# The weighted accumulation of a mixture-of-experts stage, on GpSimd in two instructions in place of one on VectorE

## The chip, the cores and the metric

The kernel runs on one core of one Trainium2 chip. Its time is the device time of the whole program in microseconds (us); a comparison takes the median of several executions. TensorE is PE in the profile, VectorE is DVE, ScalarE is ACT, GpSimd is POOL, SyncE is SP.

## The reference

One decoder layer over `x` of 2 x 256 tokens by 128 features: self-attention, a second attention with a causal and a cross part, and an expert stage, each followed by a residual and a layer norm. The change touches the expert stage alone:

```python
gate_scores = softmax(einsum('btd,ed->bte', x, Wg))
topk_val, topk_idx = top_k(gate_scores, 2)
topk_val = topk_val / (topk_val.sum(-1, keepdims=True) + 1e-9)
comb = (one_hot(topk_idx, 8) * topk_val[..., None]).sum(-2)
out = zeros_like(x)
for e in range(8):
    h = einsum('btd,hd->bth', x, W1[e]) + b1[e]        # 512 columns
    a, b = split(h, 2, axis=-1)
    eo = einsum('bth,dh->btd', a * sigmoid(b), Wo) + bo
    out = out + eo * comb[..., e:e + 1]
x = layernorm(x + out)
```

All experts share `Wo`, so the kernel sums `a * sigmoid(b)` over the experts with the weights of `comb`, and multiplies by `Wo` once.

## The kernel before

The kernel is written engine by engine, with semaphores. A function `plan()` makes one list of steps, `steps`, and each engine's block walks this list in order and issues its own part of each step. So the order of the steps is the order in every engine's queue, and an instruction that waits holds back all that stands behind it on its engine.

The two batches (b = 0, 1) have two token tiles of 128 each (t = 0, 1). The steps of the expert stage are:

- `GATE b`: TensorE makes the gate's logits, ScalarE their exponentials, and VectorE goes through some twenty small instructions (L784 to L811) that end in `comb`, the weight of each token for each expert, kept in `gate[:, b, 10]`.
- `F b e t`: one expert for one token tile, 32 in all. TensorE multiplies the tile with `w1T` (L600, two records by the two parts of an fp32 product) and adds the bias (L601). The result stands in PSUM, in `w0` or `w1` for even e and in `t0` or `t1` for odd e, so four products can be on their way. ScalarE takes the tanh of one half into `tanh_b` (L926; sigmoid is written with tanh, and the factor of one half is in the weights), which has four slots. VectorE makes the gated product `(tanh + 1) * a` into `gated` (L819, the rows call it `val_qc`), which has two slots, and frees the PSUM buffer. Then it adds the product times its weight to `gsum` (the rows call it `ctx_room`): L832 for e = 0, L835 for the seven others.
- `GT b t`: TensorE transposes the finished sum (L608), VectorE copies it out of PSUM (L840).
- `OUT b t`: TensorE multiplies by `Wo` (L615), VectorE adds the residual (L844) and takes the variance (L641, L644), GpSimd raises it to the power -0.5 (L995, L996), and VectorE normalizes (L651). SyncE stores.

`m` is one PSUM buffer for all of transposes, gate and output products; the next of them waits until VectorE has emptied it.

The items F are counted n = 0 to 31 in the order of the list. It runs: n = 0 to 7 are batch 0, tile 0, with the last attention steps of batch 1 among them (`TY`, `YT` and `WO`: its values normalized by L732, L734 and L737, transposed by L552, multiplied by L560; then the layer norm `LN`, L651 twice, behind n = 7). Items 8 and 9 are batch 0, tile 1, e = 0 and 1. Then `XT` (transpose, copied out by L760) and `GATE` of batch 1. Items 10 to 17 are batch 1, tile 0; 18 and 19 are batch 1, tile 1, e = 0 and 1; `GT 0 0`; 20; `GT 1 0`; 21; `OUT 0 0`; 22 to 26 (batch 0, tile 1); `OUT 1 0`; 27 to 31 (batch 1, tile 1); `GT 0 1`; `OUT 0 1`; `GT 1 1`; `OUT 1 1`.

GpSimd has nothing to do in this stage but L995 and L996.

## Time and profile before

| | us |
|---|---|
| median of 3 runs (271.98 to 272.28) | 272.1 |
| the profiled execution: from its first to its last instruction (its span) | 266.8 |
| the median less this span | 5.3 |
| busy in the span: PE / DVE / ACT / POOL | 195.4 / 176.4 / 91.5 / 57.7 |
| the expert items F, from the first L600 to the last product | 197.6 to 257.1 |

For the profiled execution the profile gives the span alone; the 5.3 us are what lies around it. Busy time is the time in which an engine executed something, and of an engine that is not the last to end a wait it says little. In the stretch from 198 us to the end, TensorE is busy nearly all the time; the rows in the last section but one show where it is not. A timeline row gives the start, the busy time, the engine and line, the operation with output <- input, and in brackets how long the engine had been idle and what ended that.

### The profile page before, as it was taken

To read this page: it belongs to the slowest core of one execution; us is meant where nothing else is said; L and a number is where in the kernel's file an instruction comes from. 1 tells how busy PE (TensorE), PEld (TensorE's weight loads), DVE (VectorE), ACT (ScalarE), POOL (GpSimd) and SP (SyncE) were. 2 spreads that over 40 slices of the span, in tenths; PEclk is the share of its full clock that TensorE was granted. 3 is DMA by queue.
4 is the path that set the end of the run, shared out by engine and by line. 5 is a ranking of instruction groups with operands and counts; after the bars stand their busy time and mean duration, and the time that the engine had idled before them with its cause. 6 is when DMAs were issued, how large, how long until landed. Compare 5 with 4: busy or idle time off the path is not lost.

```text
span 266.8 us, 3648 instructions
## 1 busy us (share of the span) xinstructions
PE 195.4 (73%) x1280; PEld 89.6 (34%) x1280; DVE 176.4 (66%) x423; ACT 91.5 (34%) x138; POOL 57.7 (22%) x85
## 2 busy tenths in 40 slices
PE   4605800878976085349978999999999997999961
PEld 2301100322335053134424343566555422233321
DVE  4999921498447089517888798897432686867762
ACT  4500000547740001013507485666765222222210
POOL 8993005940136017500000000001000010001101
PEclk9855555599999579559989999999999997999995
DMA  6339998000016645840000000000000000000000
GB/s 147 50 55 101 117 142 345 4 0 4 2 24 56 61 43 72 75 35 4 2 2 0 4 0 2 2 4 2 6 0 2 0 0 4 0 0 11 8 2 20
DMA packets 8117, 9.41 MB, mean 35 GB/s; under 512 B 1380, under 2 KB 6940, under 8 KB 7972
## 3 DMA queue, kind: packets, MB, share of 16 engines
q1 hardware_dynamic: 6660, 6.82, 14.8%
q0 software_dynamic: 1440, 2.37, 8.1%
q8 instruction: 10, 0.16, 0.3%
q14 instruction: 7, 0.06, 0.1%
HBM read 4.02 MB, written 0.26 MB: 16 GB/s over the span
## 4 chain that ended last, share of the span: by engine, by line
PE 51%; DVE 24%; DMA 16%; issue 3%; SPq 3%; ACT 2%; POOL 0%; POOLq 0%; ACTq 0%; DVEq 0%
PE y L527 11%; DVE mneg L694 11%; DMA q_stack_A<-mrow 6%; PE t L600 6%; PE w L600 6%; PE w L451 4%; DMA k_stack_b<-part_k 4%; PE t L496 4%; DMA q_stack_B<-mrow 4%; DVE part_q L634 3%; SPq L377 2%; PE t L478 2%; PE t L485 2%; PE w L601 2%; PE t L601 2%
## 5 line engine op out<-in xcount | busy, mean ns | idle before, releaser
L694 DVE TENSOR_REDUCE mneg<-w 128x1 f32<-128x512 f32 (+2 forms) x128 | 78.4, 651 | 38.8 <-PE w L441 14.8
L886 ACT ACTIVATE probs<-t 128x1024 f32<-128x1024 f32 x48 | 48.4, 1023 | 64.6 <-PE t L478 41.6
L995 POOL TENSOR_SCALAR rstd<-mv 128x2 f32<-128x2 f32 (+1 forms) x8 | 1.8, 224 | 165.3 <-DVE mv L644 165.3
L441 PE MATMUL w<-k_stack_a,q_stack_A 128*128 128x256 bf16 x64 | 16.3, 363 | 20.3 <-DMA q_stack_A<-part_q 15.7
L451 PE MATMUL w<-k_stack_c,q_stack_A 128*128 128x512 bf16 x64 | 25.1, 409 | 4.1 <-DVE mneg L694 3.5
L883 ACT ACTIVATE probs<-t 128x768 f32<-128x768 f32 x16 | 12.8, 810 | 24.2 <-PE t L490 24.2
L496 PE MATMUL t<-q_stack_A,k_stack_c 128*128 128x256 bf16 x128 | 19.7, 278 | 0.4 <-ACT probs L886 0.3
L527 PE MATMUL y<-probs,v_c 128*32 128x256 f32 x256 | 19.0, 388 | 0.3 <-issue 0.2
L600 PE MATMUL t<-w1T,xT 128*128 128x512 f32 x32 | 18.5, 660 | 0.0
L600 PE MATMUL w<-w1T,xT 128*128 128x512 f32 x32 | 18.2, 652 | 0.0
L441 PEld LDWEIGHTS w<-k_stack_a,q_stack_A 128*128 128x128 bf16 x64 | 5.1, 111 | 33.1 <-DMA q_stack_A<-part_q 17.0
L444 PE MATMUL w<-k_stack_b,q_stack_B 128*128 128x128 bf16 x32 | 7.7, 240 | 11.0 <-DMA k_stack_b<-part_k 7.6
L478 PE MATMUL t<-q_stack_A,k_stack_a 128*128 128x512 bf16 x32 | 10.8, 432 | 6.6 <-DMA q_stack_A<-mrow 6.5
L485 PE MATMUL t<-q_stack_B,k_stack_b 128*128 128x256 bf16 x32 | 9.6, 300 | 7.5 <-DMA q_stack_B<-mrow 7.2
L835 DVE SCALAR_TENSOR_TENSOR ctx_room<-val_qc,gate,ctx_room 128x256 f32<-128x256 f32 x28 | 13.6, 486 | 1.0
L496 PEld LDWEIGHTS t<-q_stack_A,k_stack_c 128*128 128x128 bf16 x128 | 11.7, 99 | 7.2 <-issue 5.0
L819 DVE SCALAR_TENSOR_TENSOR val_qc<-val_qk,w 128x256 f32<-128x256 f32 x16 | 6.7, 420 | 9.6 <-ACT val_qk L926 9.5
L926 ACT ACTIVATE val_qk<-t 128x256 f32<-128x256 f32 x16 | 6.1, 383 | 18.6 <-PE t L601 18.6
L451 PEld LDWEIGHTS w<-k_stack_c,q_stack_A 128*128 128x128 bf16 x64 | 6.2, 98 | 18.2 <-DVE mneg L694 13.6
L819 DVE SCALAR_TENSOR_TENSOR val_qc<-val_qk,t 128x256 f32<-128x256 f32 x16 | 6.7, 417 | 8.3 <-ACT val_qk L926 8.2
L926 ACT ACTIVATE val_qk<-w 128x256 f32<-128x256 f32 x16 | 6.1, 383 | 17.0 <-PE w L601 17.0
L897 ACT ACTIVATE y_sb<-y 128x512 f32<-128x512 f32 x12 | 7.2, 596 | 11.3 <-PE y L527 11.2
(168 smaller groups left out, 336.6 us busy)
## 6 DMA issues: line engine op xcount, KB each, us to landing
w1T<-in_w1T SPq DMA_DIRECT2D x1, 2048.0 KB, 19.5
k_stack_c<-y_sb POOLq DMA_DIRECT2D x6, 256.0 KB, 12.3
rest<-in_rest SPq DMA_DIRECT2D x1, 772.0 KB, 15.4
q_stack_A<-part_q SPq DMA_DIRECT2D x12, 64.0 KB
q_stack_B<-part_q SPq DMA_DIRECT2D x12, 64.0 KB
bias_row<-in_rows SPq DMA_DIRECT2D x1, 384.0 KB, 7.3
k_stack_b<-part_k POOLq DMA_DIRECT2D x6, 64.0 KB, 6.2
k_stack_b<-part_k SPq DMA_DIRECT2D x6, 64.0 KB
```

The source lines that it names most:

```text
L441: last = nc.tensor.matmul(o[:, i * T:(i + 1) * T], q[:, head, q0 + i * P:q0 + (i + 1) * P], k_stack_a[:, q0:q0 + T], start=True, stop=True)
L451: last = nc.tensor.matmul(o[:], q[:, head, q0 + qt * P:q0 + (qt + 1) * P], k_stack_c[:, head, b * TC:(b + 1) * TC], start=True, stop=True)
L478: last = nc.tensor.matmul(o[:, kt * 512:(kt + 1) * 512], k_stack_a[:, q0 + kt * P:q0 + (kt + 1) * P], rhs, start=True, stop=True)
L485: nc.tensor.matmul(o[:, c0:c0 + T], k_stack_b[:, head, q0:q0 + P], q[:, head, q0:q0 + T], start=True, stop=False)
L496: last = nc.tensor.matmul(o[:, kt * T:(kt + 1) * T], k_stack_c[:, head, k0:k0 + P], q[:, head, q0:q0 + T], start=True, stop=True)
L527: last = nc.tensor.matmul(y_open[32 * j:32 * j + VW, cols], v, p, start=(kt == 0), stop=(kt == last_kt[part]), tile_position=(0, 32 * j))
L600: nc.tensor.matmul(o, x2T[:, b * T + t * P:b * T + (t + 1) * P], w1T[:, e, :], start=True, stop=False)
L694: emptied(V.tensor_reduce(out=dst, in_=src, axis=AX.X, op=ALU.max, negate=True), s)
L819: emptied(V.scalar_tensor_tensor(out=product, in0=tanh_b[:, n % 4, :], scalar=1.0, in1=o[:, 0:HF], op0=ALU.add, op1=ALU.mult), s)
L835: ins = V.scalar_tensor_tensor(out=dst, in0=product, scalar=weight, in1=dst, op0=ALU.mult, op1=ALU.add)
L883: ins = A.activation(dst.rearrange("p (i c) -> p i c", i=2)[:, :, 0:T + P], o[:].rearrange("p (i c) -> p i c", i=2)[:, :, 0:T + P], ACT.Exp)
L886: ins = A.activation(dst, o[:], ACT.Exp)
```

## The change

VectorE keeps the gated product (now L823) and no longer weighs or adds. GpSimd does it: for e = 0 one multiplication by the weight into the sum, for the seven others a multiplication into a scratch tile `weighed` (in the old room of `part_qc`) and an addition to the sum. Each of GpSimd's pair waits for the one before. Four waits are new: GpSimd waits for the product (the semaphore that also frees the PSUM buffer), for `comb` at e = 0, and after each addition for itself; VectorE waits, before the product of item n, until GpSimd has finished item n - 2, since `gated` has two slots.

```diff
+        weighed = part_qc[:, 0:2, :].bitcast(F32).rearrange("p a n -> p (a n)").rearrange("p (a n) -> p a n", n=HF)
...
-                    link(V.tensor_tensor(t["comb"], t["one0"], t["one1"], ALU.add))
+                    V.tensor_tensor(t["comb"], t["one0"], t["one1"], ALU.add).then_inc(s_comb, 1)
+                    dve.wait_ge(s_comb, b + 1)
...
+                    if n >= 2:
+                        dve.wait_ge(s_gated, n - 1)
...
-                    wait_emptied(dve, s)
-                    dst = gsum[:, b, t, :]
-                    weight = gate[:, b, 10, t, e:e + 1]
-                    if e == 0:
-                        ins = V.tensor_scalar(dst, product, weight, None, ALU.mult)
-                    else:
-                        dve.wait_ge(s_gated, n)
-                        ins = V.scalar_tensor_tensor(out=dst, in0=product, scalar=weight, in1=dst,
-                                                     op0=ALU.mult, op1=ALU.add)
-                    ins.then_inc(s_gated, 1)
...
+                elif kind == "F":
+                    _, b, e, t = s
+                    n = f_of[s[1:]]
+                    wait_emptied(pool, s)
+                    if n == 0:
+                        pool.wait_ge(s_stack["qC0"], STACKED)
+                        pool.wait_ge(s_stack["qC1"], STACKED)
+                    dst = gsum[:, b, t, :]
+                    weight = gate[:, b, 10, t, e:e + 1]
+                    if e == 0:
+                        pool.wait_ge(s_comb, b + 1)
+                        G.tensor_scalar(dst, gated[:, n % 2, :], weight, None, ALU.mult).then_inc(s_gated, 1)
+                    else:
+                        link(G.tensor_scalar(weighed[:, n % 2, :], gated[:, n % 2, :], weight, None, ALU.mult))
+                        G.tensor_tensor(dst, dst, weighed[:, n % 2, :], ALU.add).then_inc(s_gated, 1)
+                        pool.wait_ge(s_gated, n + 1)
```

The queue of VectorE from `GT 1 0` to item 22, before. `part_k<-m` is the copy of `GT 1 0`, `z`, `stats`, `mv` and `rest` are `OUT 0 0`:

```order
L819 SCALAR_TENSOR_TENSOR val_qc<-val_qk,w0 128x256 [waits full_w0,tanh_done]
L835 SCALAR_TENSOR_TENSOR ctx_room<-val_qc,gate,ctx_room 128x256 [waits gated_sum,free_w0]
L840 COPY part_k<-m 128x256 [waits full_m]
L819 SCALAR_TENSOR_TENSOR val_qc<-val_qk,w1 128x256 [waits full_w1,tanh_done]
L835 SCALAR_TENSOR_TENSOR ctx_room<-val_qc,gate,ctx_room 128x256 [waits gated_sum,free_w1]
L844 TENSOR_TENSOR z<-m,xpb 128x128 [waits full_m]
L641 BN_STATS stats<-z 128x6 [waits free_m]
L644 BN_AGGR mv<-stats 128x2 [waits chain_dve]
L651 TENSOR_SCALAR rest<-z,mv,rstd 128x128 [waits rstd]
L819 SCALAR_TENSOR_TENSOR val_qc<-val_qk,t1 128x256 [waits full_t1,tanh_done]
L835 SCALAR_TENSOR_TENSOR ctx_room<-val_qc,gate,ctx_room 128x256 [waits gated_sum,free_t1]
```

The same place of VectorE's queue with the change, down to the same item:

```order
L823 SCALAR_TENSOR_TENSOR val_qc<-val_qk,w0 128x256 [waits gated_sum,full_w0,tanh_done]
L834 COPY part_k<-m 128x256 [waits full_m]
L823 SCALAR_TENSOR_TENSOR val_qc<-val_qk,w1 128x256 [waits gated_sum,full_w1,tanh_done]
L838 TENSOR_TENSOR z<-m,xpb 128x128 [waits full_m]
L642 BN_STATS stats<-z 128x6 [waits free_m]
L645 BN_AGGR mv<-stats 128x2 [waits chain_dve]
L652 TENSOR_SCALAR rest<-z,mv,rstd 128x128 [waits rstd]
L823 SCALAR_TENSOR_TENSOR val_qc<-val_qk,t1 128x256 [waits gated_sum,full_t1,tanh_done]
```

The three L835 are gone, and each product waits for `gated_sum`, the count that GpSimd now makes.

GpSimd's queue from the same `OUT 0 0` on, before: the pairs of three `OUT` steps follow each other, and each waits for its own variance.

```order
L995 TENSOR_SCALAR rstd<-mv 128x1 [waits variance]
L996 TENSOR_TENSOR rstd<-rstd,half_neg 128x1 [waits chain_pool]
L995 TENSOR_SCALAR rstd<-mv 128x1 [waits variance]
L996 TENSOR_TENSOR rstd<-rstd,half_neg 128x1 [waits chain_pool]
L995 TENSOR_SCALAR rstd<-mv 128x1 [waits variance]
L996 TENSOR_TENSOR rstd<-rstd,half_neg 128x1 [waits chain_pool]
```

With the change, GpSimd's queue from item 20 to item 23 (`free_w0` and the like are the product's semaphores, `variance` is that of `OUT 0 0`):

```order
L1005 TENSOR_SCALAR part_qc<-val_qc,gate 128x256 [waits free_w0,gated_sum]
L1006 TENSOR_TENSOR ctx_room<-ctx_room,part_qc 128x256 [waits chain_pool]
L1005 TENSOR_SCALAR part_qc<-val_qc,gate 128x256 [waits free_w1,gated_sum]
L1006 TENSOR_TENSOR ctx_room<-ctx_room,part_qc 128x256 [waits chain_pool]
L989 TENSOR_SCALAR rstd<-mv 128x1 [waits variance,gated_sum]
L990 TENSOR_TENSOR rstd<-rstd,half_neg 128x1 [waits chain_pool]
L1005 TENSOR_SCALAR part_qc<-val_qc,gate 128x256 [waits free_t1]
L1006 TENSOR_TENSOR ctx_room<-ctx_room,part_qc 128x256 [waits chain_pool]
L1005 TENSOR_SCALAR part_qc<-val_qc,gate 128x256 [waits free_w0,gated_sum]
L1006 TENSOR_TENSOR ctx_room<-ctx_room,part_qc 128x256 [waits chain_pool]
```

The power of `OUT 0 0` now stands behind item 21 on GpSimd, that of `OUT 1 0` behind item 26, and that of `OUT 0 1` behind item 31; before, nothing stood ahead of them.

## Rows read from the trace of the kernel before

**Rows 1.** One window: busy PE, PEld, DVE, ACT, POOL (instructions), granted clock, DMA, GB/s

```profile
230.00:238.00 8.00, 8.00 (x19) 2.09 (x18) 5.60 (x13) 2.19 (x6) 0.00 (x0) 1.00 0.00 0
```

**Rows 2.** Timeline (start, us, what): two of TensorE's items, VectorE's sum

```profile
231.09 1.12 PE L600 MATMUL t<-w1T,xT 128*128 128x512 f32 x2
232.47 1.12 PE L600 MATMUL w<-w1T,xT 128*128 128x512 f32 x2
233.50 0.48 DVE L835 SCALAR_TENSOR_TENSOR ctx_room<-val_qc,gate,ctx_room 128x256 f32<-128x256 f32 x1
```

**Rows 3.** Timeline, VectorE ahead of the transpose of batch 1's attention

```profile
209.16 0.42 DVE L819 SCALAR_TENSOR_TENSOR val_qc<-val_qk,w 128x256 f32<-128x256 f32 x1 [1.29 <-ACT val_qk L926]
210.86 0.42 DVE L737 TENSOR_TENSOR ytok<-ytok 128x256 f32<-128x256 f32 x1
```

**Rows 4.** Timeline, from item 9 to the gate's product of batch 1

```profile
221.24 0.48 DVE L835 SCALAR_TENSOR_TENSOR ctx_room<-val_qc,gate,ctx_room 128x256 f32<-128x256 f32 x1
221.64 0.42 DVE L760 COPY xT<-m 128x256 f32<-128x256 f32 x1
222.21 0.58 PE L590 MATMUL m<-rest,xT 128*128 128x8 f32 x4 [1.56 <-DVE xT L760]
```

**Rows 5.** Timeline, from item 19 to `GT 1 0`

```profile
239.00 0.48 DVE L835 SCALAR_TENSOR_TENSOR ctx_room<-val_qc,gate,ctx_room 128x256 f32<-128x256 f32 x1
239.40 0.42 DVE L840 COPY part_q<-m 128x256 f32<-128x256 f32 x1
239.96 0.41 PE L608 MATMUL m<-ident,ctx_room 128*128 128x128 f32 x2 [0.39 <-DVE part_q L840]
```

**Rows 6.** Timeline, GpSimd: an addition and a cast of 256 columns

```profile
78.28 0.67 POOL L941 TENSOR_TENSOR val_qk<-val_qk,part_k 128x256 f32<-128x256 f32 x1 [3.67 <-ACT val_qk L912]
79.02 0.47 POOL L942 CAST part_k<-val_qk 128x256 bf16<-128x256 f32 x1
```

**Rows 7.** GpSimd's groups by form: busy us, mean ns of one

```profile
L1003 POOL TENSOR_TENSOR xpb<-x,bias_row 128x128 f32<-128x128 f32 x4 | 1.7, 455 | 9.3 <-DVE x L651 9.3
L995 POOL TENSOR_SCALAR rstd<-mv 128x2 f32<-128x2 f32 x4 | 0.9, 227 | 120.9 <-DVE mv L644 120.9
```

**Rows 8.** VectorE, a cast in the timeline and L832 among its groups

```profile
77.97 0.29 DVE L634 CAST part_q<-val_qk 128x256 bf16<-128x256 f32 x1
L832 DVE TENSOR_SCALAR ctx_room<-val_qc,gate 128x256 f32<-128x256 f32 x4 | 1.4, 354 | 0.1
```

**Rows 9.** Timeline, from item 21 through `OUT 0 0` to item 22

```profile
242.06 0.42 DVE L819 SCALAR_TENSOR_TENSOR val_qc<-val_qk,w 128x256 f32<-128x256 f32 x1 [0.70 <-ACT val_qk L926]
243.84 0.23 POOL L995 TENSOR_SCALAR rstd<-mv 128x1 f32<-128x1 f32 x1 [27.20 <-DVE mv L644]
244.76 0.34 DVE L651 TENSOR_SCALAR rest<-z,mv,rstd 128x128 f32<-128x128 f32 x1 [1.00 <-POOL rstd L996]
245.02 0.41 DVE L819 SCALAR_TENSOR_TENSOR val_qc<-val_qk,t 128x256 f32<-128x256 f32 x1
```

**Rows 10.** Timeline, GpSimd at `OUT 1 0`

```profile
251.16 0.22 POOL L995 TENSOR_SCALAR rstd<-mv 128x1 f32<-128x1 f32 x1 [6.43 <-DVE mv L644]
```

**Rows 11.** Timeline, the copy of `GT 0 1` and the norm of `OUT 0 1`

```profile
257.55 0.42 DVE L840 COPY part_q<-m 128x256 f32<-128x256 f32 x1
260.65 0.34 DVE L651 TENSOR_SCALAR rest<-z,mv,rstd 128x128 f32<-128x128 f32 x1 [0.98 <-POOL rstd L996]
```

**Rows 12.** Timeline, a VectorE cast beside a GpSimd memset

```profile
4.87 6.92 POOL L961 MEMSET k_stack_c<- 128x8192 f32 x1
6.25 6.84 DVE L634 CAST part_q<-val_qk 128x256 bf16<-128x256 f32 x1
```

**Rows 13.** TensorE's window behind the gate (busy, granted clock, DMA, GB/s)

```profile
222.90:226.50 3.60, 3.60 (x5) 0.53 0.02 7
```

**Rows 14.** Timeline, one of TensorE's items in that window, and product 10

```profile
224.74 1.99 PE L600 MATMUL t<-w1T,xT 128*128 128x512 f32 x2
227.30 0.42 DVE L819 SCALAR_TENSOR_TENSOR val_qc<-val_qk,w 128x256 f32<-128x256 f32 x1
```

More of the change, by code:

```diff
@@ L333, in build @@
         s_ytok, s_xres, s_var, s_rstd, s_xn = map(sem, ("y_normed", "residual_ready", "variance", "rstd", "x_normed"))
-        s_lmax, s_tanh, s_gated, s_fin, s_store = map(
-            sem, ("gate_max", "tanh_done", "gated_sum", "fin_ready", "stored"))
+        s_lmax, s_comb, s_tanh, s_gated, s_fin, s_store = map(
+            sem, ("gate_max", "gate_weights", "tanh_done", "gated_sum", "fin_ready", "stored"))
         block = stack.enter_context(nc.Block())
```

## The prediction

> **What bounds the kernel now.** I read the slices of the whole span first, then the chain of work that ended last, then the list of waits, and at last the timeline of the expert stage. The chain shows that the stage from 212 us on is TensorE's: in the window from 230 to 238 us TensorE is busy for 8.00 of 8.00 us, VectorE for 5.60, GpSimd for nothing [rows 1]. An item F starts every 1.38 us on TensorE (232.47 less 231.09), and VectorE's part of it, product and sum, takes some 0.9 us [rows 2]. So there the sum that the change takes off VectorE is hidden, and its removal brings nothing. It counts only where TensorE waits for VectorE with a sum in front. The waits and the timeline show four such places: ahead of the transpose of batch 1's attention [rows 3], at the gate's product [rows 4], at GT 1 0 [rows 5], and in the tail, from the copy of GT 0 1 at 257.55 on, where VectorE, TensorE and GpSimd follow each other without cover [rows 11]. A fifth kind of place is the norm in OUT, where VectorE waits 1.00 us for GpSimd's power [rows 9].
>
> **What is removed.** 28 sums L835 of 0.48 us and four L832 of 0.354 us leave VectorE [rows 2, 8]. Of these 15 us, the path sees:
> - Gate: L760 would start at 221.24, where L835 stood, in place of 221.64, and TensorE, idle for 1.56 us and released by it, starts 0.40 us earlier [rows 4].
> - GT 1 0: L840 starts at 239.00 in place of 239.40, again 0.40 us, since TensorE waits 0.39 us for it [rows 5].
> - Ahead of the transpose of batch 1's attention L737 (start 210.86) could come 0.40 us earlier. Against this stands a lock. At the kernel's start a VectorE cast that elsewhere takes 0.29 us [rows 8] took 6.84 us, from 6.25 on, and ended about 1.3 us behind a GpSimd memset that ran from 4.87 for 6.92 us [rows 12]: a VectorE operation of some kinds stands still beside a busy GpSimd. L737 has two inputs in SBUF. Product 2 ends at 209.58 [rows 3]; GpSimd's pair for it would run until about 210.95, so L737 would end near 211.3 where it ended at 211.28. I take +0.05 us here (bounds: -0.40 without a lock, +0.15 with it).
>
> The Trainium skill (SBUF — State Buffer, Who interferes with whom) says that the pair of ports that VectorE and GpSimd share is an exclusive lock, taken by a VectorE instruction with two SBUF inputs or in a two-port mode, and that the loser stands still for a whole instruction. The trace agrees in the 6.84 us; without the rule the sum would be 0.4 us lower. Products read PSUM and one SBUF tensor, so by that page they never take the lock.
>
> **What is added on GpSimd.** Per item, a multiplication by a per-token weight, 128x256, and an addition of two fp32 tiles of the same size. The addition: with 128 columns 0.455 us, and a fixed part of 0.227 us from an operation on two columns [rows 7], so 2 x 0.455 - 0.227 = 0.68 us; the addition of 256 columns with one bf16 input took 0.67 [rows 6]. Between dependent instructions lie 0.07 us (78.95 to 79.02) [rows 6]; I take 0.08 ahead of the addition and 0.07 behind. The multiplication by a weight that is read from memory is not in the trace on GpSimd. Its lower bound is the fixed 0.227 us and 254 columns at the memset's 0.84 ns (6.92 us for 8192): 0.44 us [rows 7, 12]. Its upper bound is the two-input addition, 0.68. Nearest is the cast of 256 columns, also one input and one output, 0.47 us [rows 6]; on VectorE the weight makes L832 0.354 where a cast takes 0.29 [rows 8], so I add 0.06 and take 0.53 us. One item then costs GpSimd r = 0.53 + 0.08 + 0.68 + 0.07 = 1.36 us, with bounds of 1.26 and 1.51. TensorE's pace is 1.38. So GpSimd is full: it follows, but can catch up on nothing.
>
> The Trainium skill (GPSIMD Engine Reference, Performance versus the Vector engine) gives a best case of about 1.8 cycles per element for a one-input loop at 1.2 GHz, and calls VectorE the engine for elementwise work. That is an estimate of 0.23 + 256 x 1.5 ns = 0.61 us for the multiplication, r = 1.44, and the sum below would be 273.4 in place of 272.5. No row here has this operation; the cast of rows 6 is cheaper than the page's rate.
>
> **What moves.** GpSimd walks the same list, so each power (L995, L996) now stands behind the item in front of it, and VectorE's norm, with the next products queued behind it, waits for both. This decides the end. I walk it in the old clock times, the shifts of TensorE left out:
> - Product 21 starts at 242.06 and ends at 242.48 [rows 9]; GpSimd has it from 242.56 to 243.92 (r). The variance is now ready 0.44 us earlier, but the power starts at 243.92, where it started at 243.84 [rows 9]. The saved sum is eaten by the wait for GpSimd.
> - From the power's start to the norm's start 0.92 us, to product 22 another 0.26 [rows 9], product and hand-over 0.50: GpSimd starts item 22 at 245.60. Items 22 to 26 queue up in front of the power of OUT 1 0: 5 x 1.36 = 6.80, so it starts at 252.40, where it started at 251.16 [rows 10]. VectorE stands in the norm for that time, with products 27 and on behind it.
> - Again 0.92 + 0.26 + 0.50 = 1.68: GpSimd starts item 27 at 254.08, and has 31 done at 260.88. Only then comes the power of OUT 0 1, and the norm 0.92 later, at 261.80. Before, it stood at 260.65 [rows 11]. VectorE's copy of GT 1 1 stands behind this norm, and the rest of the kernel behind the copy.
>
> In short, the norm of OUT 0 1 comes at 246.84 + 11 r. With r = 1.36 that is 1.15 us late, although the copy of GT 0 1 alone would have come 0.40 early. Four PSUM buffers hide all this from TensorE: item 31 needs the buffer of item 27, and product 27 ends near 254.0, before TensorE comes to item 31. For item 10 the new wait for comb costs nothing, since VectorE makes both in order. The four e = 0 items cost GpSimd one instruction (0.60 us), by which the small backlog behind the layer norm and the gate is worked off ahead of item 20.
>
> **The sum.** -0.40 (gate) - 0.40 (GT 1 0) + 0.05 (transpose) + 1.15 (tail) = +0.40 us. The profiled span of 266.8 becomes 267.2, and with the 5.3 us around it the median of 272.1 becomes 272.5.
>
> **The rivals.**
> - **GpSimd is slower than TensorE's pace.** The multiplication costs as much as the two-input addition: r = 1.51, the norm at 263.45, 2.80 us late, sum +2.05, time 274.1. For it: GpSimd does this in a software loop, and one more operand must be fetched. Against it: the cast. It decides from r = 1.37 on, where the sum passes +0.54. Anything at or above a multiplication of 0.54 us is measurably slower.
> - **The pair is cheap.** With r = 1.26 the norm stands at 260.70, 0.05 late, and the sum is -0.70: 271.4. The turn from faster to slower is at r = 1.32, a multiplication of 0.49 us.
> - **The clock stays up.** Behind the gate's wait of 1.56 us TensorE's granted clock was 0.53 for 3.60 us [rows 13], that is mostly at 1.2 in place of 2.4 GHz, and two matmuls took 1.99 us [rows 14] where they take 1.12 [rows 2]. At full clock the same work takes 1.9 us, so up to 1.7 us, some 1.4 on the path, are lost there. The wait shortens to 1.16 us, and the drop may not come. GpSimd would give back a part: product 10 is bound to the gate's chain on VectorE (227.30, now 226.90) [rows 14], and from 227.40 GpSimd has ten pairs and two single items to the power of OUT 0 0, 14.8 us, until 242.2; the forecast has 243.92 - 0.80 = 243.1. So 0.9 us at r = 1.36: 271.6. With r = 1.26 all of the 1.4 would count, 270.0.
> - **VectorE's saving isn't on any path**, and GpSimd keeps up: no change, 272.1. The two waits of rows 4 and 5 speak against it; it falls within the same band.
>
> **Chances.** Forecast (multiplication of 0.47 to 0.57 us, clock as before) 0.34; slow GpSimd 0.32; cheap pair 0.18; clock 0.13; something else that costs, such as more locking, 0.03. A change of less than 0.2% (0.54 us) can't be told from none. Faster: most of the clock case and half of the cheap pair, 0.21. Slower: the slow case, and the upper part of the forecast's own span, 0.42. Within 0.2%: the rest, 0.37. The range reaches from the clock case with a cheaper pair, 270.9, to the slow case with 0.5 us of blocking more, 274.6.
>
> **What would show it.** Right: GpSimd about 97% busy from item 22 to 31 with r near 1.36, the multiplication at 0.53 us, the power of OUT 1 0 and OUT 0 1 directly behind an addition, VectorE idle for more than 2 us in the norm of OUT 1 0, the gate's product 0.4 us earlier. Wrong: a multiplication far from 0.53, or TensorE held by a full PSUM buffer in the stage's middle, or a granted clock of 1.00 behind the gate.

## The result

The changed kernel takes 281.3 us (279.7 to 284.7, 4 runs) where the kernel before took 272.0 on the same chip (271.5 to 272.3, 4 runs): ratio 1.035, 95% interval 1.025 to 1.044. The prediction was 272.5 with a range of 270.9 to 274.6. It named the right side and the right places in the tail, and was far too small: an instruction was sized too cheap, and with its real size GpSimd sets the pace in a stretch where the prediction let TensorE lead.

Executions of one kernel differ here by several us, some faster and some slower, and much of this lies ahead of the expert stage, which starts anywhere from 196.5 to 202.6 us in the fourteen profiles. So the experiments are read by the **stage**: from the start of the first expert product on TensorE (L600, in the changed kernel L601) to the start of the last norm (L651, now L652). Before, 197.62 to 264.52 = 66.9 us; changed, 196.45 to 275.14 = 78.7 us, so 11.8 us more. (The two spans, 266.8 and 277.4 us, differ by 10.6, since this stage starts 1.2 us earlier.) A second trace of the changed kernel, and one of the kernel before with instructions added ahead of the stage, give 78.7 and 66.9 again.

One thing varies in the stage beside the change: how long TensorE stays at the lower of its two clock levels (1.2 in place of 2.4 GHz) behind the gate. It is 3.4 us in the kernel before and 6.8 in the changed one; two kernels below that differ in little else show what 3.4 us more of it cost where TensorE leads: 1.7 us. A difference between two stages of that size says nothing before the clock has been looked at.

The groups of GpSimd in the changed kernel, by form (busy us, mean ns of one | idle time before them and its releaser):

```profile
L1005 POOL TENSOR_SCALAR part_qc<-val_qc,gate 128x256 f32<-128x256 f32 x28 | 26.0, 928 | 11.5 <-DVE val_qc L823 9.8
L1006 POOL TENSOR_TENSOR ctx_room<-ctx_room,part_qc 128x256 f32<-128x256 f32 x28 | 20.3, 726 | 2.3
L1003 POOL TENSOR_SCALAR ctx_room<-val_qc,gate 128x256 f32<-128x256 f32 x4 | 3.7, 926 | 19.2 <-DVE val_qc L823 19.0
```

The multiplication by the weight takes 0.93 us, where the prediction took 0.53 and at most 0.68. The addition, 0.73, is near the 0.68 that was worked out. The timeline of GpSimd and VectorE in the stretch that answers to [rows 1] and [rows 2]:

```profile
230.91 0.92 POOL L1005 TENSOR_SCALAR part_qc<-val_qc,gate 128x256 f32<-128x256 f32 x1 [0.33 <-DVE val_qc L823]
...
232.74 0.92 POOL L1005 TENSOR_SCALAR part_qc<-val_qc,gate 128x256 f32<-128x256 f32 x1
233.75 0.72 POOL L1006 TENSOR_TENSOR ctx_room<-ctx_room,part_qc 128x256 f32<-128x256 f32 x1
...
234.60 0.42 DVE L823 SCALAR_TENSOR_TENSOR val_qc<-val_qk,t 128x256 f32<-128x256 f32 x1 [1.18 <-POOL ctx_room L1006]
```

A pair starts every 232.74 - 230.91 = 1.83 us (0.93 + 0.08 + 0.72 + 0.10), against TensorE's pace of 1.38 [rows 2], and VectorE waits for GpSimd before a product. The next view gives one long window, with the columns of [rows 1]: from item 10's instruction on GpSimd to the power of `OUT 0 1`.

```profile
227.90:270.25 42.35, 33.90 (x78) 11.30 (x78) 13.32 (x37) 8.04 (x21) 36.41 (x46) 0.86 0.01 3
```

GpSimd is busy for 36.4 of 42.35 us. The rest is four waits, 2.4 us together, and the short gaps between its 46 instructions. TensorE, which had no idle time there before but at `GT` and `OUT`, is idle for 8.4 us. The list of waits from 204 us on says the same (total us, times, longest):

```profile
DVE val_qc L823 <- POOL ctx_room L1006: 16.1, 12, 1.7
...
DVE rest L652 <- POOL rstd L990: 7.7, 4, 3.4
PEld m L616 <- DVE part_q L834: 4.9, 1, 4.9
PE m L616 <- DVE part_q L834: 4.7, 1, 4.7
```

And the chain that ended last, shares of the whole span by engine; POOL had no share in it before:

```profile
PE 40%; DVE 22%; DMA 15%; POOL 13%; issue 4%; SPq 2%; ACT 2%; POOLq 0%; another core or an unknown queue 0%; DVEq 0%; ACTq 0%
```

**Where the 11.8 us arise.** The powers and norms are the marks, in the timeline of the changed kernel. They answer to [rows 9 to 11]:

```profile
248.64 0.23 POOL L989 TENSOR_SCALAR rstd<-mv 128x1 f32<-128x1 f32 x1
...
259.50 0.23 POOL L989 TENSOR_SCALAR rstd<-mv 128x1 f32<-128x1 f32 x1
...
270.34 0.22 POOL L989 TENSOR_SCALAR rstd<-mv 128x1 f32<-128x1 f32 x1
...
271.25 0.34 DVE L652 TENSOR_SCALAR rest<-z,mv,rstd 128x128 f32<-128x128 f32 x1 [1.55 <-POOL rstd L990]
```

Counted from the stage's start, the power of `OUT 0 0` is at 52.19 us (before 46.22), 5.97 late. To the power of `OUT 1 0` it takes 10.86 us (before 7.32), 3.54 more, and to that of `OUT 0 1` 10.84, 2.24 more. Each of the three powers starts right behind an addition. So the two stretches of five items cost about what the walk gives with r = 1.83 in it (0.92 + 0.26 + 0.50 + 5 x 1.83 = 10.83). The 5.97 us ahead of item 22 are what the walk didn't hold.

There, already the gate comes late, in the rows that answer to [rows 4]:

```profile
221.05 0.42 DVE L823 SCALAR_TENSOR_TENSOR val_qc<-val_qk,t 128x256 f32<-128x256 f32 x1 [1.40 <-POOL ctx_room L1006]
221.39 0.42 DVE L761 COPY xT<-m 128x256 f32<-128x256 f32 x1
...
221.95 0.86 PE L591 MATMUL m<-rest,xT 128*128 128x8 f32 x4 [2.73 <-DVE xT L761]
```

The copy is no longer behind a sum, but behind product 9, which waits for GpSimd's item 7. TensorE waits 2.73 us in place of 1.56, and its product is 0.91 us later from the stage's start (25.50, before 24.59). Product 10, behind the gate's chain, is 1.2 us late (227.32 - 196.45 = 30.87; before 29.68 by [rows 14]). From there the items 10 to 21 go through GpSimd at its own pace, with a single wait of 0.33 us, and take 4.8 us more than before; so the longer low clock of TensorE can't have cost more than that third of a microsecond here. At `GT 1 0` [rows 5] the same thing happens:

```profile
241.92 0.42 DVE L823 SCALAR_TENSOR_TENSOR val_qc<-val_qk,t 128x256 f32<-128x256 f32 x1 [1.41 <-POOL ctx_room L1006]
242.26 0.42 DVE L834 COPY part_q<-m 128x256 f32<-128x256 f32 x1
...
242.82 0.66 PE L609 MATMUL m<-ident,ctx_room 128*128 128x128 f32 x2 [1.92 <-POOL ctx_room L1003]
```

TensorE waits 1.92 us where it waited 0.39.

### The profile page after: what moved, and what is told of

Same layout as the page of the kernel before. It is cut to its first block, busy times and chain, and to the rows that moved or that the text cites. A ratio compares the mean times of both kernels' runs of the same rounds, so it can differ in the third digit from the quotient of the medians.

```text
span 277.4 us, 3673 instructions
## 1 busy us (share of the span) xinstructions
PE 197.6 (71%) x1272; PEld 91.5 (33%) x1280; DVE 162.7 (59%) x391; ACT 91.4 (33%) x138; POOL 107.8 (39%) x145
## 4 chain that ended last, share of the span: by engine, by line
PE 40%; DVE 22%; DMA 15%; POOL 13%; issue 4%; SPq 2%; ACT 2%; POOLq 0%; another core or an unknown queue 0%; DVEq 0%; ACTq 0%
DVE mneg L695 11%; PE y L528 10%; POOL part_qc L1005 6%; DMA q_stack_A<-mrow 6%; POOL ctx_room L1006 5%; DMA k_stack_b<-part_k 4%; DMA q_stack_B<-mrow 4%; PE t L497 4%; PE w L601 3%; PE w L452 3%; DVE part_q L635 3%; SPq L378 2%; PE t L479 2%; PE t L486 2%; PE t L601 2%
## 5 line engine op out<-in xcount | busy, mean ns | idle before, releaser
L1005 POOL TENSOR_SCALAR part_qc<-val_qc,gate 128x256 f32<-128x256 f32 x28 | 26.0, 928 | 11.5 <-DVE val_qc L823 9.8
L452 PE MATMUL w<-k_stack_c,q_stack_A 128*128 128x512 bf16 x56 | 21.2, 390 | 4.6 <-DVE mneg L695 4.0
L1006 POOL TENSOR_TENSOR ctx_room<-ctx_room,part_qc 128x256 f32<-128x256 f32 x28 | 20.3, 726 | 2.3
L601 PE MATMUL w<-w1T,xT 128*128 128x512 f32 x32 | 20.3, 719 | 0.0
L601 PE MATMUL t<-w1T,xT 128*128 128x512 f32 x32 | 19.4, 692 | 0.4 <-DVE val_qc L823 0.4
L823 DVE SCALAR_TENSOR_TENSOR val_qc<-val_qk,t 128x256 f32<-128x256 f32 x16 | 6.7, 421 | 19.5 <-POOL ctx_room L1006 9.9
L823 DVE SCALAR_TENSOR_TENSOR val_qc<-val_qk,w 128x256 f32<-128x256 f32 x16 | 6.7, 421 | 19.4 <-ACT val_qk L920 12.9
L479 PE MATMUL t<-q_stack_A,k_stack_a 128*128 128x512 bf16 x32 | 10.6, 426 | 6.4 <-DMA q_stack_A<-mrow 6.4
```

The costliest lines, as they stand in the source:

```text
L452: last = nc.tensor.matmul(o[:], q[:, head, q0 + qt * P:q0 + (qt + 1) * P], k_stack_c[:, head, b * TC:(b + 1) * TC], start=True, stop=True)
L479: last = nc.tensor.matmul(o[:, kt * 512:(kt + 1) * 512], k_stack_a[:, q0 + kt * P:q0 + (kt + 1) * P], rhs, start=True, stop=True)
L601: nc.tensor.matmul(o, x2T[:, b * T + t * P:b * T + (t + 1) * P], w1T[:, e, :], start=True, stop=False)
L823: emptied(V.scalar_tensor_tensor(out=product, in0=tanh_b[:, n % 4, :], scalar=1.0, in1=o[:, 0:HF], op0=ALU.add, op1=ALU.mult), s)
L1005: link(G.tensor_scalar(weighed[:, n % 2, :], gated[:, n % 2, :], weight, None, ALU.mult))
L1006: G.tensor_tensor(dst, dst, weighed[:, n % 2, :], ALU.add).then_inc(s_gated, 1)
```

## The experiments

The expectations name four theories. A: GpSimd's time per item, 1.83 us against TensorE's pace of 1.38, makes the loss. B: GpSimd's and VectorE's memory accesses slow each other. C: the powers, queued behind items, make it. D: the added waits and the queue order cost, however long an instruction takes.

### The changed kernel again

No edit.

> The changed kernel once more, for the spread of its time and a second trace. Theory A (GpSimd's throughput: an item costs it 1.83 us, more than TensorE's 1.38) expects the multiplication at 0.92 us and the addition at 0.72 again, whatever the state of the rest, and a time of 279 to 283 us. Theory B (the two engines disturb each other on the memory ports, so that the multiplication is stretched) expects multiplications that vary with what VectorE does beside them. Theory C (the powers behind the items are what costs) expects most of the loss in VectorE's waits for the power.

Measured: 280.7 us (279.8 to 285.0), ratio 1.037 (1.023 to 1.052), stage 78.7 us, L1005 928 ns, L1006 726, as theory A expects. The stage repeats to 0.1 us.

### A constant in place of the weight

```diff
-                        link(G.tensor_scalar(weighed[:, n % 2, :], gated[:, n % 2, :], weight, None, ALU.mult))
+                        link(G.tensor_scalar(weighed[:, n % 2, :], gated[:, n % 2, :], 0.125, None, ALU.mult))
```

(L1003 likewise.) The gate's weights are left out of the sum.

> The weight read from memory is replaced by the constant 0.125 in GpSimd's multiplication, which leaves the gate's weights out of the sum; everything else is as in the changed kernel. If the fetch of the per-token weight is what makes the multiplication 0.92 us, it falls to 0.45 to 0.55 us, an item to some 1.35 us and the time to 272 to 273 us (theory A with the price of the forecast). If the operation costs that much with any second operand, the time stays at 280. Theory B expects it to stay near 0.92, since VectorE does the same beside it.

Measured: 280.4 us (277.7 to 284.0), stage 75.7, 3.0 less. The group of L1005 by form:

```profile
L1005 POOL TENSOR_SCALAR part_qc<-val_qc 128x256 f32<-128x256 f32 x28 | 23.9, 853 | 10.9 <-DVE val_qc L823 9.3
```

The weight from memory costs 0.075 us, about the 0.06 that the prediction added for it. The other 0.85 us is what the instruction costs with no second operand at all. So "one input and one output" was the wrong likeness.

### The weight as a second tensor

```diff
-                        link(G.tensor_scalar(weighed[:, n % 2, :], gated[:, n % 2, :], weight, None, ALU.mult))
+                        link(G.tensor_tensor(weighed[:, n % 2, :], gated[:, n % 2, :], weight.to_broadcast([P, HF]), ALU.mult))
```

(L1003 likewise.) The same values, in another form of instruction.

> GpSimd multiplies with a tensor operation in which the weight is read as a tensor of step 0, in place of the operation with a per-token scalar. The outputs are the same. Theory A: the multiplication costs what the addition does, 0.72 us, an item 1.62 us in place of 1.83; with some 21 items in the chain that is 3 to 4 us less, 276 to 277.5 us. Theory B: two tensors to read, so no cheaper, 280 or more. Theory C: no change worth naming.

Measured: 276.5 us (271.4 to 277.3), ratio 1.023 (1.014 to 1.033), stage 69.5.

```profile
L1005 POOL TENSOR_TENSOR part_qc<-val_qc,gate 128x256 f32<-128x256 f32 x28 | 17.3, 617 | 12.3 <-DVE val_qc L823 10.8
```

0.62 us in place of 0.93, so r = 0.62 + 0.08 + 0.72 + 0.08 = 1.50: the prediction's rival of a slow GpSimd, which had r = 1.51 and 2.05 us of loss. The stage shows 2.6, and from power to power 9.15 and 9.16 us (walk: 1.68 + 5 x 1.50 = 9.18). 9.2 of the 11.8 us go with one change of form. The profiled execution is the fastest of the five; the medians of the whole time, 276.5 and 280.7, show some 4 us of it. Theory A had the form at 0.72 us and r at 1.62: the direction was right, the price again taken from a likeness.

### The powers ahead of the item

```diff
+            pool_steps = list(steps)
...
+                if s in (("WO", 1, 1), ("OUT", 0, 0), ("OUT", 1, 0), ("OUT", 0, 1)):
+                    at = pool_steps.index(s)
+                    f = max(i for i in range(at) if pool_steps[i][0] == "F")
+                    pool_steps.insert(f, pool_steps.pop(at))
```

> On GpSimd alone, the power of four norms (of batch 1's attention and of the first three output steps) is put ahead of the item that stood in front of it; nothing else changes. Theory C: the loss goes with it, 273 to 275 us. Theory A: GpSimd's items still take their time, only the idle 0.8 us behind two powers and the last norm's wait for item 31 go, 2 to 3 us less, 277 to 279 us.

Measured: 283.7 us (282.8 to 286.6), stage 80.6, that is 1.9 us more than the changed kernel, where theory C had 273 to 275 us and theory A, which missed too, 277 to 279. GpSimd now stands still for the variance instead:

```profile
POOL rstd L995 <- DVE mv L645: 6.3, 3, 3.6
```

C falls: here GpSimd has no time to spare, and what it waits for in front of its work is lost. (The low clock behind the gate lasted 10.2 us in this profile, so the 1.9 us may not all be the order's.)

### VectorE multiplies, GpSimd adds

```diff
+                    V.tensor_scalar(weighed[:, n % 2, :], product, gate[:, b, 10, t, e:e + 1], None,
+                                    ALU.mult).then_inc(s_weighed, 1)
...
+                    if e == 0:
+                        G.tensor_copy(dst, weighed[:, n % 2, :]).then_inc(s_gated, 1)
+                    else:
+                        pool.wait_ge(s_gated, n)
+                        G.tensor_tensor(dst, dst, weighed[:, n % 2, :], ALU.add).then_inc(s_gated, 1)
```

> VectorE keeps the multiplication by the weight (into the scratch tile), GpSimd does the addition alone, and a copy for e = 0. The outputs are the same. Theory A: an item costs GpSimd 0.72 + 0.1 = 0.8 us, well under TensorE's 1.38, and VectorE 0.42 + 0.35 us; so nothing of the 9 us is left, 271.5 to 273 us, and TensorE is busy for the whole of a stretch in the stage's middle. Theory B (the engines disturb each other): VectorE's multiplication, which runs at two columns per cycle, meets GpSimd's addition in every item, and 3 us or more of the loss stay. Theory C (order): the powers stand behind the items as before, so most of the loss stays.

Measured: 271.2 us (10 runs), ratio 1.002 (0.997 to 1.007), stage 68.0. GpSimd has the same 28 additions of 0.724 us and the loss is gone but for 1.1 us, all of it there at the power of `OUT 0 0`; TensorE's low clock behind the gate lasted 6.8 us in this profile, which by itself is worth more. Theory B in its weak form is visible: VectorE's 32 multiplications take 352 to 642 ns, 388 on the mean, where L832 takes 354 alone [rows 8]. It costs no time that can be told.

### A probe of GpSimd's instructions in its idle time

In the kernel before, ahead of the stage, six operations on 64, 128 and 256 columns:

```diff
+                        for c in (64, 128, 256):
+                            a, o, q = first[0][:, 0:c], probe[:, 0:c], first[0][:, 256:256 + c]
+                            link(G.tensor_scalar(o, a, half_neg[:, 0:1], None, ALU.mult))
...
+                            link(G.tensor_tensor(o, a, half_neg[:, 0:1].to_broadcast([P, c]), ALU.mult))
+                            link(G.tensor_tensor(o, a, q, ALU.add))
+                            link(G.tensor_copy(o, a))
```

> The kernel before, with operations added on GpSimd where it is idle (behind 110 us), each waiting for the one before, at 64, 128 and 256 columns: multiplication by a per-partition scalar, by a constant, addition of a constant, multiplication by a tensor of step 0, addition of two tensors, copy. Theory A (the multiplication by a scalar is a slow loop of its own): 0.92, 0.85 and 0.85 us at 256 columns with nothing of weight beside it on VectorE, growing by more than 2 ns per column; the tensor forms 0.62 and 0.7, the copy 0.45. Theory B (stretched by VectorE's memory traffic): below 0.6 here, since VectorE reads PSUM at that time. The time of the kernel is not the question; some 13 us of GpSimd's idle time are used, and it should stay that of before.

Measured, by form (L1025 is the first line, L1028 to L1030 the last three):

```profile
L1025 POOL TENSOR_SCALAR probe<-first,half_neg 128x256 f32<-128x256 f32 x1 | 0.9, 927 | 0.1
...
L1029 POOL TENSOR_TENSOR probe<-first 128x256 f32<-128x256 f32 x1 | 0.7, 726 | 0.1
L1028 POOL TENSOR_TENSOR probe<-first,half_neg 128x256 f32<-128x256 f32 x1 | 0.6, 612 | 0.1
L1025 POOL TENSOR_SCALAR probe<-first,half_neg 128x128 f32<-128x128 f32 x1 | 0.6, 606 | 0.1
...
L1030 POOL COPY probe<-first 128x256 f32<-128x256 f32 x1 | 0.4, 397 | 0.1
```

The durations are those of the changed kernel to the nanosecond or two, though VectorE does other work here: B falls as a cause of the 0.93 us. Between 128 and 256 columns a TENSOR_SCALAR grows by 0.32 us, 2.5 ns a column; two tensors by (726 - 452) / 128 = 2.1 ns; the copy by (397 - 290) / 128 = 0.84 ns. Among these forms the copy is the cheapest by far (as the cast of [rows 6] is, 0.47 us), and TENSOR_SCALAR, which reads one tensor, is the slowest.

### The multiplication alone

```diff
-                        link(G.tensor_scalar(weighed[:, n % 2, :], gated[:, n % 2, :], weight, None, ALU.mult))
-                        G.tensor_tensor(dst, dst, weighed[:, n % 2, :], ALU.add).then_inc(s_gated, 1)
+                        G.tensor_scalar(dst, gated[:, n % 2, :], weight, None, ALU.mult).then_inc(s_gated, 1)
                         pool.wait_ge(s_gated, n + 1)
```

> The changed kernel without its 28 additions: GpSimd multiplies every product by its weight straight into the sum, in the same places of its queue and with the same waits; the sum over the experts is left out, the last expert's product stands for it. An item then costs GpSimd 0.93 us and 0.10 of hand-over, 1.03 us, though each multiplication takes as long as in the changed kernel. Theory A (GpSimd's time per item against TensorE's pace of 1.38 us, from the gate on): below the pace nothing is left of the loss; the stage from the first expert product to the last norm, 78.7 us in the changed kernel and 66.9 in the kernel before, takes 65.5 to 67.0, and the two gains of 0.4 us of the prediction (gate, GT 1 0) show. Theory B (VectorE is disturbed by GpSimd's memory accesses): GpSimd makes half of its instructions, so half of the loss stays, 71 to 74 us. Theory D (the waits between the two engines and the order of the queues cost, whatever an instruction takes): over 69 us.

Measured: 268.8 us, ratio 0.989 (0.981 to 0.996), stage 63.7, less than A's 65.5 to 67.0. All 28 slow multiplications are there (931 ns), and the loss has gone: D falls, and so does a B that would slow VectorE with every instruction of GpSimd. The gate's product starts 0.8 us earlier from the stage's start (23.82, before 24.59), with a wait of 1.05 us, and behind it the clock didn't fall, which brings the rest; see below.

### A copy in place of the multiplication

```diff
-                        link(G.tensor_scalar(weighed[:, n % 2, :], gated[:, n % 2, :], weight, None, ALU.mult))
+                        link(G.tensor_copy(weighed[:, n % 2, :], gated[:, n % 2, :]))
```

> The changed kernel with a copy of the product in place of its multiplication by the weight in the 28 pairs; the weights of experts 1 to 7 are left out of the sum. A copy of 256 columns takes GpSimd 0.40 us, so a pair takes 0.40 + 0.08 + 0.72 + 0.10 = 1.30 us. This is the case that the prediction's walk is made for, a pair a little below TensorE's pace of 1.38 us: the norm of OUT 0 1 at 246.84 + 11 x 1.30 = 261.14, 0.5 us late, and the sum -0.4 - 0.4 + 0.05 + 0.5 = -0.25 us. Theory A (the walk was right and only the multiplication was mis-sized): the stage takes 66.2 to 67.3 us (before 66.9, changed 78.7). Theory D (the structure of the pairs costs): over 68.5 us.

Measured: 269.6 us, ratio 0.994 (0.987 to 1.001), stage 67.8, half a microsecond above A's range. Copy 398 ns, addition 724, r = 1.30. From power to power 8.01 and 8.15 us (walk: 1.68 + 5 x 1.30 = 8.18). The clock was low for 6.8 us behind the gate, 3.4 us longer than before. By the 1.7 us that this costs elsewhere (an estimate here), the stage would be at 66.1, where the walk has 66.6. So with r below the pace the prediction's walk holds within half a microsecond.

### The first items, and the last ten

Two complements on the kernel before. The edit of one; the other has `n < 22 and s[2] > 0`.

```diff
+        MOVED = list(range(22, 32))
...
+                    if n in MOVED:
+                        continue
...
+                elif kind == "F" and f_of[s[1:]] in MOVED:
...
+                    G.tensor_scalar(weighed[:, n % 2, :], gated[:, n % 2, :], weight, None,
+                                    ALU.mult).then_inc(s_moved, 1)
+                    pool.wait_ge(s_moved, MOVED.index(n) + 1)
+                    pool.wait_ge(s_sum[(b, t)], e)
+                    G.tensor_tensor(dst, dst, weighed[:, n % 2, :], ALU.add).then_inc(s_sum[(b, t)], 1)
```

> The kernel before, with the two GpSimd instructions of the change for items 22 to 31 alone; items 0 to 21 are weighed and added by VectorE in one instruction. The walk of the prediction from the power of OUT 0 0 on, with r = 1.83 measured in the changed kernel: power of OUT 1 0 at 243.84 + 1.68 + 5 x 1.83 = 254.67 (before 251.16), power of OUT 0 1 at 265.50, its norm at 266.42 (before 260.65), 5.8 us late. Theory A: the stage takes 66.9 + 5.8 = 72.7 us (72 to 73.5). A rival in which only the whole run of 32 items matters (a backlog that fills up ahead of item 22 and is only handed on behind it) has 67 to 69 us here.

Measured, last ten: 277.5 us (276.8 to 281.2), ratio 1.022 (1.014 to 1.030), stage 74.2.

```profile
250.33 0.23 POOL L1007 TENSOR_SCALAR rstd<-mv 128x1 f32<-128x1 f32 x1 [28.42 <-DVE mv L649]
...
261.18 0.23 POOL L1007 TENSOR_SCALAR rstd<-mv 128x1 f32<-128x1 f32 x1
```

From power to power 10.85 and 10.84 us: with ten items alone each stretch costs what it costs in the changed kernel, 5.8 us together. Of the 7.3 us the other 1.5 lie ahead of item 22, where the instructions are those of the kernel before; there the clock was low for 6.8 us in place of 3.4. That is also why the stage is above the 72 to 73.5 that were expected.

> The complement of the kernel with the last ten: items below 22 with e > 0 by GpSimd's two instructions, all others by VectorE. In the changed kernel the power of OUT 0 0 starts 5.97 us later than before, counted from the stage's first matmul, and the ten items behind it add 5.82. Theory A: what stands ahead of item 22 is a loss of its own, about 6 us, part of which the products behind may catch up, because VectorE and TensorE are then free again: stage 71 to 73 us (before 66.9, changed 78.7), and the losses of the two halves add up to about 11.8. The prediction's walk, which held TensorE to lead until item 21, gives 66.9 + 0.5 - 0.8 = 66.6 us here.

Measured, first items: 272.4 us (271.7 to 274.0), ratio 1.005 (0.998 to 1.011), stage 70.5. The power of `OUT 0 0` is 4.5 us late from the stage's start, the end 3.6. Not all of this is GpSimd's pace. The low clock behind the gate lasted 10.2 us here in place of 3.4, and while it did, GpSimd waited for slow products:

```profile
230.16 0.92 POOL L1020 TENSOR_SCALAR part_qc<-val_qc,gate 128x256 f32<-128x256 f32 x1 [0.36 <-POOL ctx_room L1024]
...
232.63 0.92 POOL L1020 TENSOR_SCALAR part_qc<-val_qc,gate 128x256 f32<-128x256 f32 x1 [0.75 <-POOL ctx_room L1024]
...
234.69 0.92 POOL L1020 TENSOR_SCALAR part_qc<-val_qc,gate 128x256 f32<-128x256 f32 x1 [0.32 <-POOL ctx_room L1024]
```

Beyond the usual hand-over of 0.10 us these three gaps are 1.1 us of the 4.5. (The view names GpSimd itself as releaser; the products, at 229.57, 232.05 and 234.10, waited for ScalarE's tanh.) From 234.69 to the power at 247.58 seven pairs follow each other without a gap, at 1.84 us each. So the middle is a loss of its own of some 3.4 us, where the walk had none, and the clock put about 1.1 on top. A said 71 to 73 for the stage; it came out just below. The two halves give 5.8 + 3.6 = 9.4 of the 11.8 us; in the changed kernel nothing could be caught up behind item 21, because GpSimd went on at its pace.

### Only where TensorE waits

The kernel before, with only items 9, 19 and 31 (the sums ahead of the gate's copy, of the copy of `GT 1 0` and of the last transposes) on GpSimd, in the form with the weight as a tensor; the code is that of the last ten, with `n in (9, 19, 31)`.

> The kernel before, with the weighing and adding of three items alone on GpSimd (9, 19 and 31: those whose sum on VectorE stood in front of the gate, of GT 1 0 and of GT 0 1), the multiplication written as a tensor operation. Theory A: GpSimd has time for one pair at each place, so each brings TensorE's wait down by the 0.40 us of the sum: 0.8 to 1.2 us faster than before. If the three waits were not VectorE's sum: no change. If the later chain takes it back (item 31 is needed by GT 1 1 1.5 us on): 0.4 to 0.8 us faster.

Measured: 270.9 us (12 runs, 267.7 to 273.5; before 272.2, 29 runs), ratio 0.995 (0.989 to 1.001), stage 65.4, 1.5 us less than before. TensorE's waits at the gate (before 1.56) and at the product of `OUT 0 1`, which needs the copy of `GT 0 1` (before 1.57):

```profile
PE m L595 <- DVE xT L765: 1.0, 1, 1.0
PE m L620 <- DVE part_q L852: 1.0, 1, 1.0
```

The gate's product starts 24.06 us after the stage's start (before 24.59), and the norm of `OUT 0 1` 0.97 us earlier than before. The other 0.5 us of the 1.5 are the clock's: the last product of the stage ran at the upper level here and at the lower one in the kernel before. First the kernel before, then this one:

```profile
261.47 1.20 PE L615 MATMUL m<-rest,part_k 128*128 128x128 f32 x4 [1.79 <-DVE part_k L840]
```

```profile
261.69 0.68 PE L620 MATMUL m<-rest,part_k 128*128 128x128 f32 x4 [1.87 <-DVE part_k L852]
```

With item 2 too:

> As the run with three items, and item 2 as well, whose sum stands in front of the transpose of batch 1's attention. In the changed kernel this transpose came without most of its wait, so the lock that the forecast put there did not cost 0.4 us: theory A expects 0.2 us more gain than with three items; with a full lock, none.

Measured: 270.6 us (12 runs), ratio 0.995 (0.990 to 1.000), stage 67.6. The profiled execution is the longest of the twelve (274.0 us), and its clock was low for 6.8 us behind the gate where that of the kernel with three items was low for 3.4. Up to there the two are alike: the gate's product starts at 24.14 and 24.06 us, with the same wait of 1.05. The power of `OUT 0 0` follows at 47.02 and 45.34: 3.4 us more of low clock cost 1.7 us. The last product at the lower level costs 0.5 more, and 1.7 + 0.5 is the whole difference of the two stages. So item 2 brought nothing (why, see the lock below).

By the stage the idea pays in this way, by 1.0 us once the clock is taken off. The whole time, which spreads by several us, has both versions half a per cent lower, at the edge of what its interval can tell.

A single instruction on GpSimd that multiplies and adds was not tried.

## Why the prediction was wrong, point by point

- **The multiplication, 0.53 us: the step that failed.** It was taken from the cast [rows 6], "also one input and one output", between bounds of 0.44 and 0.68. It took 0.93. The upper bound failed as well: it took an instruction with two inputs to be dearer than one with a single input, and nothing in the trace said so. The row that was there and was of the same operation, L995 TENSOR_SCALAR on two columns [rows 7], gave only the fixed part. With r = 1.83 the prediction's own formula, 246.84 + 11 r, gives 266.97, 6.3 us late, and a sum of about 5.6; the runs show 11.8 in the stage.
- **"I walk it in the old clock times", with product 21 at 242.06: the second step that failed.** That TensorE leads until item 21 holds for r up to 1.38. Above it, every item from the gate on is GpSimd's; the walk then begins at product 10, and what it lacks is the 5.97 us at the power of `OUT 0 0`: 1.2 up to product 10, 4.8 from there. The copy for the weight (r = 1.30) keeps to the walk within 0.5 us, the weight as a tensor (1.50) is off by 0.7, and the kernel with the last ten shows that from `OUT 0 0` on the walk is right to 0.02 us.
- **Gate -0.40 and GT 1 0 -0.40.** True as a mechanism, but only while GpSimd is ahead of its queue: the kernel with three moved items has them (the gate 0.5 us earlier, and no wait at `GT 1 0`). In the changed kernel the place of the sum in front of the copy was taken by a wait of 1.40 us for GpSimd. The prediction saw a small backlog behind the layer norm and the gate, "worked off ahead of item 20". With r = 1.83 nothing is worked off: the layer norm's power takes GpSimd from 214.47 to 215.48, and the backlog of the items behind it is what the gate's copy waits for.
- **The lock, +0.05.** The mechanism is real, and the changed kernel missed it by luck. There VectorE's step of the transpose, which answers to [rows 3], starts 0.20 us ahead of GpSimd's addition and keeps its 0.42 us:

```profile
208.65 0.92 POOL L1005 TENSOR_SCALAR part_qc<-val_qc,gate 128x256 f32<-128x256 f32 x1 [1.13 <-DVE val_qc L823]
...
209.45 0.42 DVE L738 TENSOR_TENSOR ytok<-ytok 128x256 f32<-128x256 f32 x1
209.65 0.81 POOL L1006 TENSOR_TENSOR ctx_room<-ctx_room,part_qc 128x256 f32<-128x256 f32 x1
```

  TensorE's transpose came 0.24 us earlier from the stage's start (13.48, before 13.72). With a multiplication near the 0.53 us of the prediction the addition would be running already, and that is so in the kernel with the weight as a tensor:

```profile
210.58 0.72 POOL L1006 TENSOR_TENSOR ctx_room<-ctx_room,part_qc 128x256 f32<-128x256 f32 x1
210.72 0.86 DVE L738 TENSOR_TENSOR ytok<-ytok 128x256 f32<-128x256 f32 x1
```

  The step takes 0.86 us and ends 0.28 behind the addition. The kernel with a copy (0.64 us) and the one with item 2 moved (0.73) show the same, with 0.28 to 0.29 us left behind the addition's end. TensorE's transpose is 0.07 us later than before with item 2 moved, and 0.20 with the weight as a tensor; the prediction had +0.05 with an upper bound of +0.15. The section Who interferes with whom of the Trainium skill (SBUF — State Buffer) says that a VectorE instruction with two inputs in SBUF contends with a GpSimd instruction that reads SBUF; these three runs agree. Beside a TENSOR_SCALAR of GpSimd the effect is smaller: the two L828 behind the gate (two inputs in SBUF as well) take 0.83 us together in the changed kernel, 0.61 before.
- **The Trainium skill's rate** (GPSIMD Engine Reference, Performance versus the Vector engine) gave 0.61 us for the multiplication. That was an estimate, from its best case and a fixed part of these rows. It pointed to the right side, and the measured 0.93 is half as much again; 0.62 us is what the form with the weight as a tensor takes.
- **The sign's bound** (from r = 1.37 on measurably slower) agrees with what was run: r = 1.30 no loss that can be told, 1.50 and 1.83 slower.
- **The clock.** It fell behind the gate again, for 6.8 us in place of 3.4. In the kernel with the multiplication alone it stayed up, and what the prediction took for this case, up to 1.4 us on the path, is of the size seen there (up to 1.8) and between the kernels with three and four moved items (1.7).

## What to carry to other kernels

Before work goes to another engine, find a row of the same operation on that engine, not one of the same number of operands; where there is none, keep a bound far above the nearest. Then compare its time per item with the pace of the engine that leads: below it, the moves of this document cost at most about a microsecond; above it, each item from the first queue on pays the difference, and the gains in front of a wait are gone. Move only those instructions that stand in front of a wait of the bounding engine: three of the 32 gave 1.0 us here. And before a difference of 1 or 2 us between two traces is explained, compare how long the clock was low in each.

## What the runs showed that was not expected

- GpSimd's TENSOR_SCALAR on 256 fp32 columns takes 0.93 us (0.85 with a constant), longer than either form with two tensors (0.73, and 0.61 to 0.62 with the weight). The same multiplication written as TENSOR_TENSOR, with the weight repeated along the row, is a third cheaper.
- **The low clock behind the gate doesn't follow from the wait alone.** Windows of TensorE there, first the multiplication alone, then the copy for the weight, then the changed kernel (columns as in [rows 13]):

```profile
223.60:227.20 3.60, 3.60 (x9) 0.92 (x8) 2.50 (x17) 1.38 (x6) 0.04 (x1) 1.00 0.03 7
```

```profile
221.90:228.50 6.60, 6.60 (x9) 1.79 (x9) 4.96 (x25) 1.26 (x5) 1.99 (x3) 0.53 0.00 1
```

```profile
222.00:229.40 7.40, 7.40 (x13) 2.38 (x13) 4.86 (x25) 1.37 (x6) 3.06 (x4) 0.54 0.01 3
```

  A granted clock of 0.53 is mostly 1.2 GHz, 1.00 is 2.4 GHz. The first two had the same wait of 1.05 us at the gate's product; one kept the clock, the other lost it for 6.8 us. The kernels with three and four moved items, with 1.05 us too, lost it for 3.4 and 6.8, the kernel before, after 1.56 us, for 3.4, and the kernel with the first items moved, after 1.92 us, for 10.2. In the changed kernel it fell a second time, from 242.2 to 249.0 us, behind the wait of 1.92 us at `GT 1 0`. From gate to power of `OUT 0 0` the multiplication alone takes 2.2 us less than the kernel before, of which 0.4 are `GT 1 0`; so the low clock costs up to 1.8 us there. What decides how long it lasts stays open.
- An execution lies 1.8 to 2.3 us above its own span (270.8 and 269.0; 279.7 and 277.4). The kernel before has executions of 268.8 us with a span of 266.8, that of its profile. So of the 5.3 us that the prediction put around this span, some 3 were that the profiled execution was faster than the median.
